# Fast-weight attention: the key-value read is solved on its coefficients instead of being held row by row, and the state is turned first

## The chip, the cores and the metric

The kernel runs on one core of one Trainium2 chip. The metric is the device time of the whole program in microseconds (us). A core has five engines with queues of their own: TensorE (PE, matmuls and transposes), VectorE (DVE), ScalarE (ACT), GpSimd (POOL) and SyncE (SP, which here only issues transfers). Each runs its instructions in the order in which they are written; semaphores are the only thing that orders one engine against another.

## The reference

A small language-model tower on 16 sequences of 128 tokens. In order: an embedding with a decayed memory and four MLP layers (`tok`), a fast-weight attention (`L0_attn`), a mixture of experts, a second attention and a second mixture of experts. The change lies in the fast-weight attention. There the scan runs over the 16 sequences (`slen` = T = 16), 128 tokens are the batch, and there are NH = 8 heads of DH = 32:

```python
def ff_step(W, inp):
    qt, kt, vt, bt = inp
    v_old = jnp.einsum('bhij,bhj->bhi', W, kt)
    W = W + (bt * (vt - v_old))[..., :, None] * kt[..., None, :]
    z = jnp.einsum('bhij,bhj->bhi', W, qt)
    return (W, z)
...
def rec_step(carry, inp):
    R, h = carry
    zt, kt, vt, bt = inp
    q_rec = jax.nn.softmax(h, axis=-1)
    v_old = jnp.einsum('bhij,bhj->bhi', R, kt)
    R = R + (bt * (vt - v_old))[..., :, None] * kt[..., None, :]
    h = zt + jnp.einsum('bhij,bhj->bhi', R, q_rec)
    return ((R, h), h)
```

The first scan (`fast`) has no feedback from its output to its queries; the second (`rec`) has: the query of step t is the softmax of the state h of step t - 1.

## The kernel before

The kernel never forms W or R. It keeps the vectors u_r = b_r (v_r - v_old) of every row r and reads with dot products: z_t is the sum over r <= t of (k_r . q_t) u_r, and u_t needs the sum over r < t of (k_r . k_t) u_r. A stage ahead (`grams`) computes all dot products on PE and moves them by DMA into `C` (SBUF tile `coefs`): for step t, entries 0 to NH-1 are the key coefficients of the fast half, NH to 2NH-1 those of the recurrent half, 2NH to 3NH-1 the query coefficients of the fast half. `UV[:, r, 0]` and `UV[:, r, 1]` hold the vectors of the two halves, 256 elements each (8 heads of 32).

The stage that matters here starts when `C` is complete. Its 16 steps are written out by hand, engine by engine:

- POOL: `row_scale(t)` (scales the coefficients and the values of row t, both halves), `held(t)` (products of the key coefficients of row t with all u_r, r < t, both halves at once, two rows in a piece), `queries(t - 1)` (products of query coefficients with u_r for a part of the rows). Four buffers each for the held and the query products.
- PE: sums such products by accumulating transposes against the identity (`turned_sum`, 128 columns of the 256 at a time): `held(t + 1)` into `held_sum`, `turn_held` turns that sum back, and `read_out` and `queries` add the products of both reads into `h_bank(t)`. `turn_state(t)` turns the finished state back to tokens in rows, `out_projection(t)` applies the output matrix.
- ACT: `held_out(t)` saves the held sum, `state(t)` saves the state to `hsT`, `exponentials(t)` is the exponential of the query softmax, `query_row(t)` copies query coefficients into PSUM.
- DVE: `query_sub(t)` (maximum and subtraction on the turned state, lines L1781 and L1783), `read_coefficients(t)` (dot products of the softmaxed state with the recurrent keys, L1797 to L1816), `products` (L1774: coefficients times u_r for up to four rows; `fast` for the first read, `rec` for the second), `out_add`, `update(t + 1)` (L1761: u = scaled value minus held sum).

A step on DVE is `query_sub(t)`, the second half of the fast products, `read_coefficients(t)`, the rec products, `out_add(t - 1)`, `update(t + 1)` and the first half of the fast products of step t + 1 (there are two halves from step 8 on; rows 4 to 7 and 12 to 15 of the fast read are POOL's). The next `query_sub` waits for the state to come back: DVE's rec products, PE `read_out`, ACT `state`, PE `turn_state`. Semaphores of note: `held_p`/`held_mm` and `query_p`/`query_mm` (POOL's products made and summed), `read_p`/`read_mm` (DVE's), `upd_done` (rows of `UV` that are final), `h_T` (state turned).

## Time and profile before

| | us |
|---|---|
| median of 3 runs | 729.44 (727.9 to 730.09) |
| the profiled execution | 727.95 |
| span of the profiled execution | 726.2 |
| the stage of the 16 steps, with the DMA wait ahead of it | about 257 to 484 of the span |

A profile row says where an engine was busy, and in brackets how long it had been idle and what released it. Matmul records are modelled at their ends, and PE's clock stands in rows as a share of full speed: 1.00 is 2.4 GHz, 0.50 is 1.2 GHz.

### The profile page before, as it was taken

How to read it: one execution, taken by the hardware profiler on the slowest of the kernel's cores; microseconds unless marked ns; L12 is line 12 of the kernel's file. 1: busy time of each engine (PE TensorE's matmuls, PEld its weight loads, DVE VectorE, ACT ScalarE, POOL GpSimd, SP SyncE). 2: the span in 40 equal slices, each digit the busy share in tenths (PEclk: the TensorE clock that was granted, in tenths of full speed). 3: DMA queues.
4: the chain of work that ended last, by engine and by line, in shares of the span. 5: the costliest groups of instructions: out<-in, count | busy, mean ns of one | idle time of the engine just before them, and what ended most of it. 6: DMA issues, size and time to landing. Idle time of an engine off the chain costs nothing.

```text
span 726.2 us, 12294 instructions
## 1 busy us (share of the span) xinstructions
PE 600.5 (83%) x4657; PEld 473.8 (65%) x4657; DVE 444.4 (61%) x1099; ACT 277.9 (38%) x500; POOL 361.0 (50%) x402
## 2 busy tenths in 40 slices
PE   6889999998987706876887778666999698899996
PEld 3657777685556605766786767553688587785776
DVE  3644343337667736889789999985443726663534
ACT  0075354437976611211110100023733436566550
POOL 1696242217208636889889999346553300001334
PEclk9999999999999965889899999978998769999999
DMA  7000000000004330000000000000000000000000
GB/s 247 1 1 1 2 1 0 1 1 1 0 1 80 74 84 21 1 1 1 0 2 1 1 0 1 1 1 1 1 1 1 1 1 2 1 2 1 6 11 14
DMA packets 10698, 10.35 MB, mean 14 GB/s; under 512 B 5904, under 2 KB 9680, under 8 KB 10384
## 3 DMA queue, kind: packets, MB, share of 16 engines
q1 hardware_dynamic: 7936, 7.54, 3.7%
q0 software_dynamic: 1984, 1.62, 1.2%
q8 instruction: 37, 0.61, 0.4%
q10 hardware_dynamic: 720, 0.41, 0.2%
q14 instruction: 21, 0.17, 0.1%
HBM read 5.70 MB, written 0.52 MB: 9 GB/s over the span
## 4 chain that ended last, share of the span: by engine, by line
PE 56%; DVE 24%; ACT 7%; issue 5%; DMA 3%; POOL 3%; SPq 2%; ACTq 0%; DVEq 0%; POOLq 0%
PE bank L1071 8%; PE bank L1059 7%; DVE features L1774 6%; DVE bank L1808 5%; PE bank L1148 5%; DVE features L1797 5%; PE bank L1359 4%; PE bank L1322 4%; PE bank L1357 3%; PE bank L1423 2%; PE bank L1139 2%; PE bank L1411 2%; PE bank L1108 2%; PE bank L1117 2%; SPq L379 2%
## 5 line engine op out<-in xcount | busy, mean ns | idle before, releaser
L1148 PE MATMUL bank<-ident,features 128*128 128x128 f32 x920 | 127.0, 298 | 65.2 <-DVE features L1774 38.8
L1148 PEld LDWEIGHTS bank<-ident,features 128*128 128x128 f32 x920 | 114.0, 155 | 75.5 <-DVE features L1774 47.4
L506 POOL TENSOR_TENSOR features<-UV,coefs 128x1024 f32<-128x1024 f32 (+1 forms) x64 | 117.4, 1857 | 17.8 <-PE bank L1148 9.2
L1774 DVE TENSOR_TENSOR features<-UV,bank 128x1024 f32<-128x1024 f32 (+3 forms) x64 | 66.2, 1065 | 0.9
L695 ACT ACTIVATE G<-bank,cols 128x512 f32<-128x512 f32 x64 | 43.3, 686 | 49.6 <-PE bank L1059 49.6
L1059 PE MATMUL bank<-xs,weights 128*128 128x512 f32 x128 | 60.0, 614 | 2.5 <-ACT xs L686 2.5
L1071 PE MATMUL bank<-weights,G 128*128 128x128 f32 x512 | 59.8, 276 | 0.0
L1071 PEld LDWEIGHTS bank<-weights,G 128*128 128x128 f32 x512 | 58.4, 192 | 0.0
L349 POOL TENSOR_SCALAR rstd<-mv 128x4 f32<-128x4 f32 x8 | 1.9, 237 | 112.2 <-DVE mv L361 112.2
L762 ACT ACTIVATE hsT<-bank 128x256 f32<-128x256 f32 x16 | 6.1, 383 | 102.0 <-PE bank L1148 102.0
L481 POOL TENSOR_TENSOR UV<-xs,rows 128x512 f32<-128x512 f32 x16 | 20.3, 1270 | 46.8 <-DVE xs L1672 46.7
L1139 PE MATMUL bank<-features 32*128 32x136 f32 x768 | 33.8, 312 | 10.3 <-DVE sx L1723 2.5
L1797 DVE TENSOR_TENSOR features<-RK,bank 128x1024 f32<-128x1024 f32 (+3 forms) x40 | 41.8, 1045 | 0.1
L1059 PEld LDWEIGHTS bank<-xs,weights 128*128 128x128 f32 x128 | 24.0, 198 | 27.4 <-issue 24.3
L1808 DVE TENSOR_REDUCE bank<-features 128x32 f32<-128x1024 f32 (+3 forms) x40 | 41.5, 1058 | 0.0
L1139 PEld LDWEIGHTS bank<-features 32*128 32x128 f32 x768 | 28.7, 205 | 15.5 <-issue 4.3
L2095 DVE TENSOR_REDUCE RK<-bank 128x4 f32<-128x512 f32 x32 | 21.9, 684 | 26.0 <-PE bank L1411 26.0
L1672 DVE TENSOR_TENSOR xs<-bank,UV 128x512 f32<-128x512 f32 x16 | 11.1, 692 | 41.0 <-PE bank L1071 38.1
L340 POOL TENSOR_SCALAR rstd<-mv 128x4 f32<-128x4 f32 x32 | 7.7, 240 | 56.8 <-DVE mv L361 55.5
L342 POOL TENSOR_TENSOR rstd<-rstd,neghalf 128x4 f32<-128x4 f32 x32 | 33.2, 1037 | 2.7
L664 POOL TENSOR_TENSOR features<-features 128x512 f32<-128x512 f32 (+2 forms) x21 | 17.1, 816 | 27.1 <-DVE features L2188 17.1
L373 DVE TENSOR_SCALAR UV<-xs,mv,rstd 128x128 f32<-128x128 f32 x48 | 13.4, 343 | 24.6 <-POOL rstd L342 24.6
(318 smaller groups left out, 1346.2 us busy)
## 6 DMA issues: line engine op xcount, KB each, us to landing
weights<-in_w SPq DMA_DIRECT2D x2, 1024.0 KB, 11.6
features<-in_tok SPq DMA_DIRECT2D x1, 768.0 KB, 5.9
weights<-in_ew SPq DMA_DIRECT2D x4, 128.0 KB, 3.0
weights<-in_ew SPq DMA_DIRECT2D x2, 256.0 KB, 2.8
coefs<-G SPq DMA_DIRECT2D x16, 25.5 KB, 3.4
rows<-in_rows SPq DMA_DIRECT2D x1, 384.0 KB, 6.6
out_h<-H SPq DMA_DIRECT2D x3, 128.0 KB, 2.0
coefs<-G POOLq DMA_DIRECT2D x14, 25.5 KB, 4.9
```

The costliest lines, as they stand in the source:

```text
L342: pool.tensor_tensor(rstd[:, k, 0:n], rstd[:, k, 0:n], neghalf[:, 0:n], ALU.pow).then_inc(s["ln_rstd"], 1)
L506: pool.tensor_tensor(out, u, co, ALU.mult).then_inc(s["held_p"], 1)
L695: act.activation(G[:, 4 * (w % 2) + f, :], up_bank(f)[:], ACT.Gelu, bias=col("b1", 4 * i + f)).then_inc(s["tok_gelu"], 1)
L1059: mm(up_bank(f)[:], w1[:, i, P * f:P * f + P], xT[:, w % 2, :], start=True, stop=True).then_inc(s["tok_up"], 1)
L1071: last = mm(down_bank(w)[:, DT * j:DT * j + DT], G[:, 4 * (w % 2) + f, P * j:P * j + P], w2[:, i, f, :], start=(f == 0), stop=(f == 3))
L1139: last = mm(bank[4 * k + j][:, GB * SL * n:GB * SL * n + GB * SL], feat[left + k][x, g, 0:T].rearrange("p s b -> p (s b)"), feat[right + k ...
L1148: last = mm(out[:, P * k:P * k + P], x[:, P * k:P * k + P], ident[:], is_transpose=True, start=first and k == 0, stop=last_ and k == n - 1 ...
L1322: mm(expert_bank(k, c, e)[:], ew1[k][r, e // 2, :], xin(k, c)[r], start=True, stop=True).then_inc(s[f"x_up{e % 2}"], 1)
L1359: last = mm(bank[4 + t % 2][:, D * e:D * e + D], g, ew2[1][:, e, :], start=True, stop=True)
L1774: dve.tensor_tensor(out, u, co.unsqueeze(3).broadcast_to([P, R, NH, DH]), ALU.mult)\
L1797: ch(dve.tensor_tensor(PD[:, j, 0:R * HB].rearrange("p (r x) -> p r x", r=R), RK[:, r0:r1_, :], e.unsqueeze(1).broadcast_to([P, R, HB]), A ...
L1808: ch(dve.tensor_reduce(bankCR[:, r0:r1_, :], PD[:, j, 0:(r1_ - r0) * HB].rearrange("p (r h j) -> p r h j", r=r1_ - r0, h=NH), AX_X, ALU.add))
```

## The change

The fast half's u_r are no longer formed. Since its queries don't depend on its outputs, the triangular system can be solved on the coefficients: `weigh_keys` scales the key coefficients of a block of rows, `eliminate` subtracts, for one row x after the other from the last to the first, (query coefficient of x) times (key coefficients of row x) from the query coefficients of rows below x, and `weigh_reads` scales the result. The fast read is then a sum over the raw values `UV[:, r, 0]`. It is done in blocks of CH = 4 steps: steps 0 to 3 on DVE (in step 0), steps 4 to 15 on POOL by the table `SOLVE`, which spreads the eliminations over POOL's steps 1 to 10. `row_scale`, `held`, `held_out`, `turn_held` and `update` deal with the recurrent half alone, and a held piece is now four rows of 256 elements instead of two of 512. DVE makes the fast products of rows 0 to 3 only, POOL all others. The order changes on every engine: PE turns the state right behind the rec read-out, POOL makes the queries of the same step, DVE does `out_add` behind `query_sub` and the whole fast product of the next step ahead of it. `expert_bias`, two products for the next stage, moves from steps 1 and 3 to steps 13 and 14 of POOL.

```diff
-READS = [x for x in read_pieces() if x[0] == "rec" or x[2] % 8 == 0]
-QUERIES = [x for x in read_pieces() if x[0] == "fast" and x[2] % 8]
-HELDS = [(t, r0, r1) for t in range(1, T) for r0, r1 in pieces(t, 2)]
+READS = [x for x in read_pieces() if x[0] == "rec" or x[2] == 0]
+QUERIES = [x for x in read_pieces() if x[0] == "fast" and x[2]]
+HELDS = [(t, r0, r1) for t in range(1, T) for r0, r1 in pieces(t)]
...
+        def weigh_keys(eng, lo, hi):
+
+            x = C[:, lo:hi, 0:NH, 0:hi]
+            return eng.tensor_tensor(x, x, bsum2[:, lo:hi, 0].unsqueeze(3).broadcast_to([P, hi - lo, NH, hi]), ALU.mult)
+
+        def eliminate(eng, ch, lo, hi, x, scratch):
+
+            t0 = max(lo, x)
+            n = hi - t0
+            full = [P, n, NH, x]
+            less = scratch[:, 0:n * NH * x].rearrange("p (t h r) -> p t h r", t=n, h=NH)
+            cq = C[:, t0:hi, 2 * NH:KD * NH, 0:x]
+            ch(eng.tensor_tensor(less, C[:, t0:hi, 2 * NH:KD * NH, x].unsqueeze(3).broadcast_to(full),
+                                 C[:, x, 0:NH, 0:x].unsqueeze(1).broadcast_to(full), ALU.mult))
+            ch.settle()
+            ch(eng.tensor_tensor(cq, cq, less, ALU.subtract))
+
+        def weigh_reads(eng, ch, lo, hi):
...
+            ch(eng.tensor_tensor(cq, cq, rsum[:, lo:hi, 2, :].unsqueeze(3).broadcast_to(full), ALU.mult))
+            ch.settle()
+            eng.tensor_tensor(cq, cq, bsum[:, 0:hi, 0, :].rearrange("p r h -> p h r").unsqueeze(1).broadcast_to(full),
+                              ALU.mult).then_inc(s["query_scaled"], 1)
...
+            SOLVE = {1: (("rows", 4, 8), ("less", 4, (7, 6, 5))),
+                     2: (("less", 4, (4, 3, 2, 1)), ("done", 4, 8)),
+                     3: (("rows", 8, 16), ("less", 8, (11, 10, 9, 8))),
+                     4: (("less", 8, (7, 6, 5, 4)),),
+                     5: (("less", 8, (3, 2, 1)), ("done", 8, 12), ("less", 12, (15, 14))),
+                     6: (("less", 12, (13, 12, 11)),),
+                     7: (("less", 12, (10, 9, 8)),),
+                     8: (("less", 12, (7, 6, 5)),),
+                     9: (("less", 12, (4, 3)),),
+                     10: (("less", 12, (2, 1)), ("done", 12, 16))}
...
             for t in range(1, T):
...
-                held(t)
-                queries(t - 1)
-                if t in (1, 3):
-                    expert_bias(t // 2)
-            queries(T - 1)
+                held(t)
+                queries(t)
+                if t == 1:
                     pool.wait_ge(s["sums_done"], 2)
+                if t in SOLVE:
+                    solve(SOLVE[t])
+                if t in (13, 14):
+                    expert_bias(t - 13)
...
             for t in range(T):
+                read_out("fast", t, reads_of("fast", t))
+                queries(t)
                 if t + 1 < T:
                     held(t + 1)
-                second_half(t)
-                if t + 1 < T:
                     turn_held(t + 1)
-                queries(t)
                 read_out("rec", t, reads_of("rec", t))
                 if t + 1 < T:
-                    first_half(t + 1)
                     turn_state(t)
                     out_projection(t)
...
             def next_query(t):
 
                 update(t)
-                dve.wait_ge(s["upd_done"], t + 1)
                 dve.wait_ge(s["query_row"], t + 1)
-                part = reads_of("fast", t)
-                products("fast", t, part[0:len(part) // 2])
+                products("fast", t, reads_of("fast", t))
 
             def step(t):
                 if t:
                     query_sub(t)
-                part = reads_of("fast", t)
-                products("fast", t, part[len(part) // 2:])
+                    out_add(t - 1)
                 read_coefficients(t)
+                dve.wait_ge(s["upd_done"], t + 1)
                 products("rec", t, reads_of("rec", t))
-                if t:
-                    out_add(t - 1)
                 if t == 0:
+                    first_reads()
                     normalisers(slice(CH, T))
-                if t == 1:
                     ch.settle()
                     strengths(slice(CH, T))
-                if t >= 2 and t + 2 < 2 * CH - 1:
-                    query_scale(t - 1)
                 if t + 1 < T:
                     next_query(t + 1)
```

Where the order moves, first on PE, step 12 of the stage. `bank<-ident,features` are the transposes that sum products (of `held`, of the fast read and of the rec read, all kept in `features`), `bank<-ident,G` those of POOL's queries, `bank<-ident,accT` is `turn_held`, `bank<-ident,hsT` is `turn_state`. Before, with 52 for `held(13)` and 8 for half of the fast read in the first row, and 26 for the rec read and 8 for the first half of step 13 in the fourth:

```order
L1148 MATMUL bank<-ident,features 128x128 x60
L1168 MATMUL bank<-ident,accT 128x128 x4
L1148 MATMUL bank<-ident,G 128x128 x10
L1148 MATMUL bank<-ident,features 128x128 x34
L1187 MATMUL bank<-ident,hsT 128x128 x2
L1195 MATMUL bank<-outw,hsT 128x64 x2
```

and of the change:

```order
L1205 MATMUL bank<-ident,features 128x128 x8
L1205 MATMUL bank<-ident,G 128x128 x18
L1205 MATMUL bank<-ident,features 128x128 x26
L1225 MATMUL bank<-ident,accT 128x128 x2
L1205 MATMUL bank<-ident,features 128x128 x26
L1244 MATMUL bank<-ident,hsT 128x128 x2
L1252 MATMUL bank<-outw,hsT 128x64 x2
```

The 26 of the rec read now stand directly ahead of `turn_state`, and the transposes of a step fall from 116 to 84.

On POOL, from `row_scale(7)` up to `row_scale(8)`. `features<-UV,coefs` is `held`, `G<-UV,coefs` is `queries`, `coefs<-coefs,bsum` and `UV<-UV,coefs` are `row_scale`. Before:

```order
L488 TENSOR_TENSOR coefs<-coefs,bsum 128x16x7
L490 TENSOR_TENSOR UV<-UV,coefs 128x512
L506 TENSOR_TENSOR features<-UV,coefs 128x1024 x3
L506 TENSOR_TENSOR features<-UV,coefs 128x512
L520 TENSOR_TENSOR G<-UV,coefs 128x768
```

and of the change, where `xs<-coefs` and `coefs<-coefs,xs` are the two operations of an `eliminate`:

```order
L514 TENSOR_TENSOR coefs<-coefs,bsum 128x8x7
L516 TENSOR_TENSOR UV<-UV,coefs 128x256
L532 TENSOR_TENSOR features<-UV,coefs 128x1024
L532 TENSOR_TENSOR features<-UV,coefs 128x768
L545 TENSOR_TENSOR G<-UV,coefs 128x1024
L388 TENSOR_TENSOR xs<-coefs 128x320
L391 TENSOR_TENSOR coefs<-coefs,xs 128x4x8x10
L388 TENSOR_TENSOR xs<-coefs 128x288
L391 TENSOR_TENSOR coefs<-coefs,xs 128x4x8x9
L388 TENSOR_TENSOR xs<-coefs 128x256
L391 TENSOR_TENSOR coefs<-coefs,xs 128x4x8x8
```

Two held products are gone, and six small products stand between the queries and the next row's `row_scale`.

On DVE, from behind the last rec product of step 12 to the start of step 13's coefficients. Before:

```order
L1857 TENSOR_TENSOR H<-bank,H 128x64
L1761 TENSOR_TENSOR UV<-UV,bank 128x512
L1774 TENSOR_TENSOR features<-UV,bank 128x1024
L1781 TENSOR_REDUCE mx<-bank 128x8
L1783 TENSOR_TENSOR dd<-bank,mx 128x256
L1774 TENSOR_TENSOR features<-UV,bank 128x1024
L1797 TENSOR_TENSOR features<-RK,bank 128x1024
```

and of the change:

```order
L1809 TENSOR_TENSOR UV<-UV,bank 128x256
L1822 TENSOR_TENSOR features<-UV,bank 128x1024
L1829 TENSOR_REDUCE mx<-bank 128x8
L1831 TENSOR_TENSOR dd<-bank,mx 128x256
L1899 TENSOR_TENSOR H<-bank,H 128x64
L1845 TENSOR_TENSOR features<-RK,bank 128x1024
```

The product between `dd` and the coefficients (L1797, now L1845) is gone, and `out_add` stands there.

## Rows read from the trace of the kernel before

**Rows 1.** Window of the stage: PE, PEld, DVE, ACT, POOL busy, clock, DMA:

```profile
257.00:484.00 227.00, 157.99 (x1176) 142.70 (x1177) 187.70 (x293) 25.73 (x63) 171.55 (x120) 0.86 0.03 8
```

**Rows 2.** Waits of DVE in the stage (us in total, times, longest us):

```profile
DVE mx L1781 <- PE bank L1187: 21.5, 15, 2.1
```

**Rows 3.** Timeline, coefficients of step 12 to coefficients of 13: start, us, engine, line:

```profile
411.43 1.21 DVE L1797 TENSOR_TENSOR features<-RK,bank 128x1024 f32<-128x1024 f32 x1
...
419.70 3.81 DVE L1774 TENSOR_TENSOR features<-UV,bank 128x1024 f32<-128x1024 f32 x4
420.97 3.57 PE L1148 MATMUL bank<-ident,features 128*128 128x128 f32 x26 [1.90 <-DVE features L1774]
...
424.58 0.38 ACT L762 ACTIVATE hsT<-bank 128x256 f32<-128x256 f32 x1 [7.47 <-PE bank L1148]
...
425.55 1.09 PE L1148 MATMUL bank<-ident,features 128*128 128x128 f32 x8 [1.01 <-DVE features L1774]
...
426.90 0.42 DVE L1781 TENSOR_REDUCE mx<-bank 128x8 f32<-128x256 f32 x1 [1.40 <-PE bank L1187]
427.09 4.54 PE L1148 MATMUL bank<-ident,features 128*128 128x128 f32 x40
...
428.83 1.21 DVE L1797 TENSOR_TENSOR features<-RK,bank 128x1024 f32<-128x1024 f32 x1
```

**Rows 4.** Timeline of DVE, ends of steps 6, 7 and 8 and what follows:

```profile
331.81 2.09 DVE L1774 TENSOR_TENSOR features<-UV,bank 128x1024 f32<-128x1024 f32 x2
...
335.88 0.42 DVE L1781 TENSOR_REDUCE mx<-bank 128x8 f32<-128x256 f32 x1 [1.26 <-PE bank L1187]
...
343.12 2.35 DVE L1774 TENSOR_TENSOR features<-UV,bank 128x1024 f32<-128x1024 f32 x2
...
349.53 0.42 DVE L1781 TENSOR_REDUCE mx<-bank 128x8 f32<-128x256 f32 x1 [2.07 <-PE bank L1187]
...
350.87 1.22 DVE L1797 TENSOR_TENSOR features<-RK,bank 128x1024 f32<-128x1024 f32 x1
...
356.85 2.68 DVE L1774 TENSOR_TENSOR features<-UV,bank 128x1024 f32<-128x1024 f32 x3
...
363.39 0.42 DVE L1781 TENSOR_REDUCE mx<-bank 128x8 f32<-128x256 f32 x1 [1.87 <-PE bank L1187]
```

**Rows 5.** Windows of 2 us, PE busy and its granted clock:

```profile
312.00:314.00 2.00, 1.80 (x9) 0.50 0.00 0
...
474.00:476.00 2.00, 0.00 (x0) 0.50 0.00 0
```

**Rows 6.** Timeline, read-outs at the low clock, steps 4 and 15:

```profile
310.13 1.55 DVE L1774 TENSOR_TENSOR features<-UV,bank 128x1024 f32<-128x1024 f32 x2
...
315.10 0.42 DVE L1781 TENSOR_REDUCE mx<-bank 128x8 f32<-128x256 f32 x1 [2.09 <-PE bank L1187]
...
475.94 4.61 DVE L1774 TENSOR_TENSOR features<-UV,bank 128x1024 f32<-128x1024 f32 x4
477.21 6.05 PE L1148 MATMUL bank<-ident,features 128*128 128x128 f32 x32 [8.19 <-DVE features L1774]
...
483.30 0.38 ACT L762 ACTIVATE hsT<-bank 128x256 f32<-128x256 f32 x1 [17.88 <-PE bank L1148]
```

**Rows 7.** Groups of POOL by shape, count | busy, mean ns | idle before:

```profile
L506 POOL TENSOR_TENSOR features<-UV,coefs 128x1024 f32<-128x1024 f32 x56 | 108.9, 1968 | 11.2 <-PE bank L1148 6.2 <-DVE UV L1761 5.0
...
L520 POOL TENSOR_TENSOR G<-UV,coefs 128x256 f32<-128x256 f32 x2 | 1.3, 634 | 0.0
...
L488 POOL TENSOR_TENSOR coefs<-coefs,bsum 128x240 f32<-128x240 f32 x1 | 0.6, 596 | 0.0
...
L488 POOL TENSOR_TENSOR coefs<-coefs,bsum 128x16 f32<-128x16 f32 x2 | 0.4, 222 | 10.1 <-DVE bsum L1745 10.1
```

**Rows 8.** DVE around the first step, and step 4's start:

```profile
272.15 1.95 DVE L1739 RECIPROCAL coefs<-coefs 128x288 f32<-128x288 f32 x1
...
304.52 0.42 DVE L1781 TENSOR_REDUCE mx<-bank 128x8 f32<-128x256 f32 x1 [1.00 <-PE bank L1187]
```

80 lines of the change are left out of this document (47 added, 33 removed).

## The prediction, on record before the changed kernel ran

> **What bounds the kernel now.** Only one stretch of the program is touched, so I first read the windows by stage: the 16 steps take 227 us with the DMA wait ahead of them, and in them DVE is busy for 188 us, POOL for 172 us and PE for 158 us [rows 1]. No engine is full, so the next view is the waits of DVE: 21.5 us in 15 waits, one per step, for the transposed state to come back from PE [rows 2]. The timeline of one step says what a step consists of [rows 3]. DVE's last rec product of step 12 ends at 423.51 (419.70 + 3.81), `query_sub` of step 13 starts at 426.90 and the coefficients of step 13 (L1797) start at 428.83. I call 423.51 to 426.90 the exit of a step (3.39 us) and 426.90 to 428.83 its entry (1.93 us). Between an entry and the next exit DVE is busy without a gap in `read_coefficients` and the rec products, and there the change alters nothing. So a step's time is entry + fixed work + exit, as long as POOL's held sum is there in time, and the change is to be judged by entries, exits and POOL.
>
> **What the change does to the entry.** The entry is maximum, subtraction and the fast product of 1.13 us (the start of the next instruction; the row says 1.21), so 0.80 us without it. The coefficients also wait for ACT's exponential. Step 8 shows that wait bare, since its product is only one row long: 1.34 us from 349.53 to 350.87 [rows 4]. After the change `out_add` (0.22 us) stands in that wait, so every entry is 1.34 us: 0.6 us less in steps 1 to 7 and 11 to 15, and in steps 8, 9 and 10, whose product is one, two and three rows long, 0, 0.1 and 0.3 us less. `out_add` costs nothing there; without the wait it would cost 0.14 us.
>
> **What it does to the exit.** At step 12 ACT saves the state at 424.58, 1.07 us after DVE's end, then PE must wait for the first half of the next fast read (1.01 us idle, 1.09 us of transposes from 425.55) before it turns the state [rows 3]. The changed order puts the turn directly behind the rec read. Step 6, which has no first half yet, shows such an exit: 333.90 to 335.88, 2.0 us [rows 4]. The update (0.34 us for half of its columns) and the fast product (1.13 us) fit into it. So 3.4 us become 2.0 us, if PE is at its full clock. Steps 4 and 15 show the price if it isn't. Step 4: 311.68 to 315.10, 3.4 us [rows 6], at a granted clock of 0.50 [rows 5]. Step 15: 32 transposes take 6.05 us from 477.21, and the state is taken 2.75 us after DVE's end at 480.55 [rows 6]; with the save, the turn and their hops (0.95 us, what step 6 has between) that is an exit of 3.7 us.
>
> **Which clock PE will have.** Before step 15's read-out PE had been idle for 8.2 us and the clock was 0.50 [rows 5, 6]; before step 12's it had been idle for 1.9 us after dense work and it was fast, 26 transposes in 3.6 us [rows 3]. At full clock 40 transposes take 4.54 us, 0.113 us each [rows 3]. In the changed step 12 PE has 8 + 18 + 26 = 52 of them, 5.9 us; with 0.5 us for turn and projection and 0.9 us for the save and turn of the held sum it is done 7.3 us after the step's start. The first rec product is ready after entry, coefficients (411.43 to 419.70, 8.3 us [rows 3]) and one product, 1.34 + 8.3 + 1.2 = 10.8 us. The idle stretch grows from 1.9 us to about 3.5 us, in steps 9 to 14 alike (3.0 to 3.8), because the held sums have half the transposes. Between the row of 1.9 us (fast) and that of 8.2 us (slow) I take the slow one as likelier: steps 7 and 8 too went slow, and there the end of the rec read was late, 345.47 to 349.53 is 4.1 us and 359.53 to 363.39 is 3.9 us, 0.5 to 0.7 us over step 12's exit [rows 3, 4]. So I take the exits of steps 4, 5 and 9 to 15 at the low clock. The Trainium skill, "TensorE: Matmul & The Clock Gate", section "A second HAM failure mode: psum-queue depth-cycling", says that short idles between groups of matmuls can make the clock swing; the trace shows both, a fast read-out behind 1.9 us of idle and slow ones. By that rule the sum below stands near 722; by the row of 1.9 us it would be 708.
>
> **POOL's sum.** Its prices: 1.97 us for a product of 1024, 0.63 for one of 256 (1.945 and 0.59 from start to start), and for small ones 0.222 us at 16 elements and 0.596 at 240 [rows 7], so 0.195 us + 1.67 ns per element; each that waits for the one ahead of it gets 0.08 us. An elimination of n elements is two of these. By `SOLVE` and the sizes in the order's rows steps 1 to 7 hold 58 such instructions with 11,500 elements: 58 x 0.275 + 11,500 x 0.00167 = 35.1 us, by step 3.3, 4.7, 6.6, 4.6, 6.4, 5.2, 4.5. Steps 8 to 10 add 9.1 us. Against that, held products fall from 120 rows of 512 to 120 of 256 elements, `row_scale` from about 1.4 us to 0.8. What a step of POOL costs (queries, solve, next row's scaling, next held) is 5.1, 7.0, 9.3, 8.5, 11.2, 10.9 and 11.2 us for steps 1 to 7, then 11.5, 10.7, 13.4, 10.6, 11.8, 14.6, 15.6. It starts at 276.8: DVE's reciprocal, at 272.15 before [rows 8], comes behind eight small products of `first_reads` (1.8 us by POOL's nearest row of 0.22 us [rows 7], having none of DVE that small beside it), and 1.95 + 0.8 us of reciprocal and strengths follow. So held(8) is complete at 276.8 + 63.2 = 340.0.
>
> DVE over the same steps, at 1.93 to 1.34 us entries. Steps 2 and 3 are POOL's: held(4) is complete at 276.8 + 21.4 = 298.2; PE sums it (8 transposes at 0.22 us, 1.8), ACT saves it and PE turns it (1.2), then come the 8 transposes of rec(3) (1.8), and save and turn of the state (1.2): step 4 starts at 304.2, where it started at 304.52 [rows 8]. The late start from `first_reads` is made good by the shorter held(2). From there on POOL is 3 to 4.5 us ahead of DVE's exits, not more: step 7's exit starts at 344.2 (345.47 less 0.3 and four entries of 0.6, more 1.4 for a slow exit of step 5, all from the sum below) and held(8) is there at 340.0, with 2.3 to 4 us of sum, save and turn to do. It is hidden, but only just, and each further us on POOL in steps 1 to 7 would show.
>
> **The sum.** Up to step 4: 0.3 us gained. Steps 4 to 7: four entries of 0.6 (2.4), step 7's exit 4.1 to 2.0 (2.1), step 5's exit 2.0 to 3.4 at the low clock, since POOL gives PE nothing for 6.4 us of its solve (-1.4): 3.1. Step 8: exit 3.9 to 2.0, 1.9 gained, as POOL's products keep PE busy right up to the read. Steps 9 to 14: exits of 3.7 instead of 3.4 (3.5 and 3.6 in 9 and 10, with fewer rows), entries 0.1, 0.3 and four times 0.6: 2.8 - 1.5 = 1.3. Step 15: entry 0.6, same end. Together 7.2 us. The profiled execution took 727.95, 1.75 us more than its span of 726.2, and nothing outside the stage changes, so 720.8; the median of the runs is 1.5 us above it, so 722.2 on that basis. I say 722.
>
> Not in the sum: `expert_bias` in steps 13 and 14 (3.8 us, hidden behind 1.6 us or more of room per step and no longer in the way of steps 1 and 3), `query_scale` gone from DVE (it lay in the exit's wait), ACT's save of 256 instead of 512 columns (in the term of the held sum).
>
> **Rivals.** *The clock stays up* (0.15). If 3.5 us of idle don't bring it down, exits in steps 4, 5 and 9 to 14 are 2.0 us and step 15's end 1.7 us shorter: 1.4 + 1.4 + 3.1 + 6.8 + 1.7 = 14.4 more, 708. For it: the idle before step 12's read was over half of that without any fall. Against it: steps 7 and 8. Mixed cases lie between.
>
> *Everything eaten* (0.16). The clock is low in steps 6 to 8 too (three times 1.4 us) or POOL is 10% dearer, and 7 us shrink to 0 to 3: 726.5 to 729.5.
>
> *POOL becomes the bound of steps 2 to 9, and the kernel slower* (0.11). The small eliminations have three free dimensions with strides and repeats, which no row shows at this size; from below they can't be under 0.22 us, from above the nearest row is that of 1024 at 1.9 ns per element, and in between lies doubt. A solve that costs half more makes held(8) complete at 357.5; with 4.6 us of sums, turns and read-out step 8 starts near 362, 12.6 us later than before, of which steps 9 to 15 give back 2 to 4: 738. It decides from about 8 us more on POOL up to step 7, 23% of 35.1. The Trainium skill, "GPSIMD Engine Reference", section "Elementwise — side-by-side cycle accounting", gives 4497 ns for 2048 elements, 2.2 ns per element where this trace has 1.9 or less at 1024. By its figure the solve up to step 7 would be some 6 us longer (an estimate from that page), and the sum would come to about 727.
>
> *The main case* (0.58): gain of 3 to 12 us, 717 to 726.
>
> **The numbers.** 0.3% (2.2 us) is about what a measurement of this kernel can tell from no change. Faster: the main case nearly whole and the high clock, 0.73. Same: most of the third case, 0.15. Slower 0.12. The range leaves out the far half of the first rival and the bound by POOL: 712 to 729.
>
> **What the profile should show.** Eliminations on POOL near 0.2 + 1.67 ns per element, one of 224 at 0.57 us. Entries of 1.34 us. `turn_state` directly behind the save, and exits of 2.0 or 3.4 to 3.7 us going with a granted clock of 1.00 or 0.50 in the read-out. PE idle for 3 to 4 us ahead of the rec read in steps 9 to 14. DVE never waiting for the held sum from step 4 on. The stage ending near 476 where it ended at 483.30. What would prove me wrong: a DVE wait at `update` after step 4, eliminations that take over 0.7 us each, or full clock throughout.

## The result: 722.2 us, and where the 6.5 us come from

The changed kernel takes 722.17 us (median of 4 runs, 720.68 to 722.83), the kernel before 728.67 us beside it (4 runs, 727.9 to 730.09): ratio 0.9906, 95% interval 0.9881 to 0.993. The forecast was 722.0. The size is right, but the profile shows that it came from terms that are partly wrong and cancel. (One traced execution, that of experiment 9, took 1035.56 us at a mean granted clock of 0.559; its exits aren't read, and that experiment's ratio comes from the five other executions.)

The profiled execution of the changed kernel took 722.83 us with a span of 721.1 us. Its window of the stage and DVE's waits in it, to be set beside [rows 1, 2]:

```profile
261.00:482.00 221.00, 136.68 (x904) 121.68 (x904) 175.77 (x289) 20.26 (x63) 159.51 (x173) 0.78 0.03 8
```

```profile
DVE mx L1829 <- PE bank L1244: 20.1, 14, 2.4
...
DVE UV L1809 <- PE bank L1225: 8.1, 4, 2.8
```

PE has some 270 transposes fewer, and its mean granted clock in the window fell from 0.86 to 0.78. DVE's wait for the turned state is almost what it was, 20.1 us after 21.5. The other wait of DVE on PE grew: four times it stands at `update` for the held sum, 8.1 us in all, the last time ahead of step 6. Before, that wait was about half as long, the last ahead of step 2:

```profile
DVE UV L1761 <- PE bank L1168: 4.4, 2, 3.3
```

The same step as [rows 3], coefficients of step 12 to coefficients of 13:

```profile
411.54 1.22 DVE L1845 TENSOR_TENSOR features<-RK,bank 128x1024 f32<-128x1024 f32 x1 [0.32 <-ACT bank L832]
...
419.81 3.81 DVE L1822 TENSOR_TENSOR features<-UV,bank 128x1024 f32<-128x1024 f32 x4
421.09 5.40 PE L1205 MATMUL bank<-ident,features 128*128 128x128 f32 x26 [3.94 <-DVE features L1822]
423.54 0.41 DVE L1809 TENSOR_TENSOR UV<-UV,bank 128x256 f32<-128x256 f32 x1
423.87 1.21 DVE L1822 TENSOR_TENSOR features<-UV,bank 128x1024 f32<-128x1024 f32 x1
...
426.52 0.38 ACT L818 ACTIVATE hsT<-bank 128x256 f32<-128x256 f32 x1 [9.86 <-PE bank L1205]
426.96 0.44 PE L1244 MATMUL bank<-ident,hsT 128*128 128x128 f32 x2 [0.47 <-ACT hsT L818]
...
427.43 0.42 DVE L1829 TENSOR_REDUCE mx<-bank 128x8 f32<-128x256 f32 x1 [2.35 <-PE bank L1244]
...
428.23 0.21 DVE L1899 TENSOR_TENSOR H<-bank,H 128x64 f32<-128x64 f32 x1
428.77 1.22 DVE L1845 TENSOR_TENSOR features<-RK,bank 128x1024 f32<-128x1024 f32 x1 [0.32 <-ACT bank L832]
```

Entry: 427.43 to 428.77, 1.34 us where it was 1.93. Turn: directly behind the save of the state. Exit: 423.62 (419.81 + 3.81) to 427.43, 3.81 us where it was 3.39. The 26 transposes of the rec read took 3.57 us before and take 5.40 us now, behind 3.94 us of idle instead of 1.90. The windows say why:

```profile
422.00:424.00 2.00, 2.00 (x11) 2.00 (x11) 2.00 (x5) 0.00 (x0) 1.96 (x2) 0.50 0.00 0
...
430.00:432.00 2.00, 2.00 (x21) 2.00 (x19) 2.00 (x3) 0.00 (x0) 2.00 (x2) 1.00 0.03 8
```

PE is busy throughout both windows, and gets 11 matmuls done at 0.50 (1.2 GHz), 21 at 1.00 (2.4 GHz). The turn-first order should have saved 1.4 us here; the low clock took it.

Cutting the stage at the starts of `query_sub` (from the first DVE instruction on the coefficients to the last save of the state) gives 216.15 us before (267.15 to 483.30) and 210.88 us after (270.79 to 481.67), so 5.3 us. I use this stage length below, because what lies outside it moved by up to 10 us between profiled executions of these kernels (505 to 515 us), with next to nothing changed there. No kernel's stage was traced twice, so how far a stage length repeats isn't known; entries and fixed work agree to 0.02 us from kernel to kernel, exits go with the clock.

### The profile page after: what moved, and what is told of

The parts are those of the page before. It is cut to its first block, busy times and chain, and to the rows that moved or that the text cites. A ratio compares the mean times of both kernels' runs of the same rounds, so it can differ in the third digit from the quotient of the medians.

```text
span 721.1 us, 11767 instructions
## 1 busy us (share of the span) xinstructions
PE 575.3 (80%) x4387; PEld 449.8 (62%) x4387; DVE 434.7 (60%) x1098; ACT 272.6 (38%) x500; POOL 349.2 (48%) x455
## 4 chain that ended last, share of the span: by engine, by line
PE 56%; DVE 17%; POOL 9%; ACT 8%; DMA 4%; issue 3%; SPq 3%; ACTq 0%; POOLq 0%; DVEq 0%
PE bank L1128 8%; PE bank L1116 7%; PE bank L1205 6%; DVE features L1845 4%; DVE bank L1856 4%; PE bank L1368 4%; PE bank L1405 4%; PE bank L1403 3%; SPq L405 3%; PE bank L1469 2%; PE bank L1165 2%; POOL features L532 2%; PE bank L1457 2%; PE bank L1174 2%; DVE features L1822 2%
## 5 line engine op out<-in xcount | busy, mean ns | idle before, releaser
L1205 PE MATMUL bank<-ident,features 128*128 128x128 f32 x628 | 102.3, 328 | 70.9 <-DVE features L1822 52.2
L1205 PEld LDWEIGHTS bank<-ident,features 128*128 128x128 f32 x628 | 91.7, 174 | 76.9 <-DVE features L1822 40.0
L532 POOL TENSOR_TENSOR features<-UV,coefs 128x1024 f32<-128x1024 f32 (+3 forms) x36 | 59.4, 1670 | 4.1 <-DVE UV L1809 4.0
L1822 DVE TENSOR_TENSOR features<-UV,bank 128x1024 f32<-128x1024 f32 (+3 forms) x56 | 58.1, 1073 | 0.7 <-ACT bank L826 0.2
L1845 DVE TENSOR_TENSOR features<-RK,bank 128x1024 f32<-128x1024 f32 (+3 forms) x40 | 41.9, 1046 | 4.8 <-ACT bank L832 4.8
L545 POOL TENSOR_TENSOR G<-UV,coefs 128x1024 f32<-128x1024 f32 (+3 forms) x24 | 39.1, 1646 | 7.2 <-PE bank L1205 7.2
```

The costliest lines, as they stand in the source:

```text
L532: pool.tensor_tensor(out, u, co, ALU.mult).then_inc(s["held_p"], 1)
L545: pool.tensor_tensor(out, u, co, ALU.mult).then_inc(s["query_p"], 1)
L1205: last = mm(out[:, P * k:P * k + P], x[:, P * k:P * k + P], ident[:], is_transpose=True, start=first and k == 0, stop=last_ and k == n - 1 ...
L1822: dve.tensor_tensor(out, u, co.unsqueeze(3).broadcast_to([P, R, NH, DH]), ALU.mult)\
L1845: ch(dve.tensor_tensor(PD[:, j, 0:R * HB].rearrange("p (r x) -> p r x", r=R), RK[:, r0:r1_, :], e.unsqueeze(1).broadcast_to([P, R, HB]), A ...
```

## The experiments

Each time is a median of 6 to 12 runs (5 for the dealt-out kernel), beside the kernel before on the same chip (728.1 us in the first four experiments, 730.1 in the next four, 728.5 in the next three, 727.7 in the last). Exits and entries are read from DVE's timeline as in the prediction; stages come from the one traced execution of each kernel, medians from all.

**1. The old kernel with nothing but the turn moved.**

```diff
                 read_out("rec", t, reads_of("rec", t))
                 if t + 1 < T:
-                    first_half(t + 1)
                     turn_state(t)
                     out_projection(t)
+                    first_half(t + 1)
```

> The kernel before with one thing moved: PE turns the state and projects it ahead of the read-out of the next step's first half. Theory (the exits carry the gain): exits of steps 10 to 14 go from 3.4 us to 2.0 us with the clock high as before, those of 7 to 9 by 0.2 to 0.7 us with the clock low, together about 8 us less: 720.5, as fast as the whole change or faster. Rival (the gain comes from the solve and the halved held sums, the turn was hidden by DVE's own update and product): no change, 728 to 729.

Measured: 717.88 us, ratio 0.9888 (0.984 to 0.9935), stage 205.85 us. Two lines moved give at least as much as the whole change: the medians are 4.3 us apart and the stages 5.0, while the intervals of the two ratios overlap. PE at the read of step 10, before and here:

```profile
387.77 2.88 PE L1148 MATMUL bank<-ident,features 128*128 128x128 f32 x22 [2.57 <-DVE features L1774]
391.75 1.09 PE L1148 MATMUL bank<-ident,features 128*128 128x128 f32 x8 [1.10 <-DVE features L1774]
392.68 0.38 PE L1187 MATMUL bank<-ident,hsT 128*128 128x128 f32 x2
```

```profile
385.57 2.88 PE L1148 MATMUL bank<-ident,features 128*128 128x128 f32 x22 [1.31 <-DVE features L1774]
388.92 0.44 PE L1187 MATMUL bank<-ident,hsT 128*128 128x128 f32 x2 [0.47 <-ACT hsT L762]
...
389.59 0.61 PE L1148 MATMUL bank<-ident,features 128*128 128x128 f32 x4
```

The read itself takes 2.88 us in both; what goes is the 1.10 us of idle and 1.09 us of transposes ahead of the turn. Exits of steps 7 to 13 are 1.90 to 2.32 us. The transposes that moved behind the turn also shorten the idle ahead of the next read (1.31 us for 2.57 in step 10). In step 8 the clock goes with it. The read, first with the eight transposes behind it and then without, before and here:

```profile
358.12 5.01 PE L1148 MATMUL bank<-ident,features 128*128 128x128 f32 x26 [2.08 <-DVE features L1774]
```

```profile
359.37 2.44 PE L1148 MATMUL bank<-ident,features 128*128 128x128 f32 x18 [1.22 <-DVE features L1774]
```

The granted clock from 360 to 362 us was 0.50 before and 1.00 here. Exits of steps 7, 8 and 9 fell by 1.96, 1.88 and 1.59 us, where I had expected 0.2 to 0.7 with the clock low as before.

**2. The changed kernel without that move**: the solve on coefficients alone.

```diff
+                if t == 0:
+                    read_out("fast", t, reads_of("fast", t))
-                read_out("fast", t, reads_of("fast", t))
                 queries(t)
...
                 if t + 1 < T:
+                    read_out("fast", t + 1, reads_of("fast", t + 1))
                     turn_state(t)
```

> The changed kernel with the turn put back behind the read-out of the next step's fast rows. Theory: each exit of steps 3 to 14 is 1.0 to 1.3 us longer, so 12 to 15 us more, about 735, slower than the kernel before. Rival (turn hidden): within 2 us of the changed kernel, 722 to 724.

Measured: 729.71 us, ratio 1.005 (1.0013 to 1.0087), stage 218.58 us: slightly slower than before, and half way between my theory (735) and the rival (722 to 724). The move costs 7.7 us of stage and not 12 to 15, since many exits of the changed kernel were slow already. Together with experiment 1 this is a square of four:

```
time (stage), us         old solve          solve on coefficients
old order                728.7 (216.15)     729.7 (218.58)
state turned first       717.9 (205.85)     722.2 (210.88)
```

The reorder is worth 7.5 and 10.8 us in the two columns. The solve on coefficients costs 1 us in one row and 4 us in the other (2.4 and 5.0 us of stage), although entries are shorter. The next two experiments look for what it costs.

**3. Dummy transposes.** The changed kernel with transposes of the identity into an unused part of a PSUM bank, in TensorE's idle time: behind the queries of steps 3, 5, 6 (16, 20, 8 of them) and behind `turn_held` in steps 9 to 14 (20) and 15 (60).

```diff
+            def keep_busy(n):
+                for _ in range(n):
+                    nc.tensor.transpose(held_sum[:, 384:512], ident[:], ident[:])
...
                     turn_held(t + 1)
+                keep_busy(IDLE_LATE.get(t, 0))
                 read_out("rec", t, reads_of("rec", t))
```

> The changed kernel with transposes of the identity into unused columns of the held sum's bank, where PE would idle: 16, 20 and 8 behind the queries of steps 3, 5 and 6, 20 behind turn_held in steps 9 to 14, 60 in step 15. They compute nothing. Theory (the exits are long because the granted clock is 0.50 in the read-out): clock 1.00 in these read-outs, exits of 9 to 14 from 2.8 to 3.9 us down to 2.0 us and the end of step 15 1.7 us earlier, together 9 to 11 us less: 711 to 713. Rival (the exits are long for another reason, such as the late held sum or ACT): 722 or more, by up to 2 us for the added work.

Measured: 708.99 us, ratio 0.9772 (0.9721 to 0.9822), stage 203.11 us. The read of step 12:

```profile
410.14 2.35 PE L1329 MATMUL bank<-ident 128*128 128x128 f32 x20
414.25 3.58 PE L1205 MATMUL bank<-ident,features 128*128 128x128 f32 x26 [1.76 <-DVE features L1832]
418.30 0.44 PE L1244 MATMUL bank<-ident,hsT 128*128 128x128 f32 x2 [0.47 <-ACT hsT L818]
```

26 transposes in 3.58 us instead of 5.40, with 2.35 us of work that computes nothing put ahead of them. Exits of steps 9 to 13 are 1.89 to 2.10 us, and the granted clock in them is 1.00: the theory. The 13.2 us between the medians are more than this clock is worth, though. The stage lost 7.8 us: steps 9 to 15 gave 9.0 us, the size expected, and steps 0 to 8 cost 1.2, with exits of 3.42, 3.12, 5.49, 3.73 and 3.33 us in steps 4 to 8 and six waits at `update` (8.7 us). Of the other 4.9 us of the traced executions 3.8 lie ahead of the stage, where the kernels are the same. Idle time right ahead of a read isn't all that counts either: step 14's read, behind 1.97 us of idle, still took 5.16 us for 30 transposes.

**4. No eliminations.** The changed kernel without the rank-one updates on POOL (its output leaves the solve's triangular part out).

```diff
-            SOLVE = {1: (("rows", 4, 8), ("less", 4, (7, 6, 5))),
+            SOLVE = {1: (("rows", 4, 8),),
...
```

> The changed kernel without the eliminations on POOL (the rows and done parts of the solve stay, so the fast reads of steps 4 to 15 lack their corrections). Theory: POOL is late in steps 1 to 7 by about what DVE waits at its update (2.8, 1.1, 1.8 and 2.5 us ahead of steps 2, 3, 4 and 6); without 34 us of eliminations these waits shrink to the turn of the held sum, 4 to 6 us less, 716 to 718. Rival (the solve is hidden, the waits come from PE's low clock): 721 to 722.

Measured: 716.57 us, ratio 0.9839 (0.9784 to 0.9894), stage 202.55 us. DVE never waits at `update`; exits of steps 1 to 7 are 1.88 to 2.98 us instead of 1.99 to 5.26, and step 8 starts 71.9 us after the stage's start instead of 81.2. Exits of steps 8 to 13 are 3.2 to 4.0 us, much as in the changed kernel (3.0 to 3.9). So POOL's lateness (9 us in steps 1 to 7) and the low clock of the later reads are two separate costs.

**5. The eliminations dealt out again**: the same ones, placed where POOL has room.

```diff
-                     2: (("less", 4, (4, 3, 2, 1)), ("done", 4, 8)),
-                     3: (("rows", 8, 16), ("less", 8, (11, 10, 9, 8))),
-                     4: (("less", 8, (7, 6, 5, 4)),),
-                     5: (("less", 8, (3, 2, 1)), ("done", 8, 12), ("less", 12, (15, 14))),
-                     6: (("less", 12, (13, 12, 11)),),
-                     7: (("less", 12, (10, 9, 8)),),
...
+                     2: (("less", 4, (4, 3, 2, 1)),),
+                     3: (("done", 4, 8), ("rows", 8, 12), ("less", 8, (11,))),
+                     4: (("less", 8, (10, 9, 8)),),
+                     5: (("less", 8, (7, 6, 5, 4)),),
+                     6: (("less", 8, (3, 2, 1)), ("rows", 12, 16), ("less", 12, (15,))),
+                     7: (("done", 8, 12), ("less", 12, (14, 13))),
...
```

> The changed kernel with its eliminations dealt out again over the steps: GpSimd's load goes from steps 1 to 3 and 5 into steps 4, 6, 7 and 11, the sum of the work unchanged. Theory A (half of what the solve part costs is GpSimd's lateness: DVE waited 2.46 us at the update ahead of step 6 and 4.75 and 4.32 us exits stand at steps 1 and 3): those exits fall to 2 to 3 us, the stage is 2 to 5 us shorter, and the time is 717 to 720 us. Theory B (the lateness is hidden behind the low clock's cold transposes, which the same exits would pay anyway): the waits at the updates go, exits stay, 721 to 723 us.

Measured: 717.88 us, ratio 0.9854 (0.9815 to 0.9893), stage 205.56 us. DVE's waits in the stage:

```profile
DVE mx L1830 <- PE bank L1245: 20.4, 14, 2.5
...
DVE UV L1810 <- PE bank L1226: 2.8, 1, 2.8
```

8.1 us of waiting for held sums have become 2.8, one wait, at step 1, and the stage is 5.3 us shorter: theory A in time and for step 3 (exit 4.32 to 2.31 us), not for step 1, whose exit stayed at 4.74. The exits of steps 3 and 5 alone gave 5.3 us. Beside them steps 4 and 7 lost 3.0 us to reads at a low clock, and steps 8 to 13 gave 2.2 us that no theory had. The solve part now costs nothing (717.9 against 717.9 in experiment 1), and gives nothing either.

**6. Both cures together**: dealt out, and dummy transposes in steps 3 to 15 (10 to 14 behind the queries of steps 3 to 8; 6 to 24 behind `turn_held` in 7 to 14 and 66 in 15).

> The same dealt-out eliminations with dummy transposes on TensorE in its idle time in steps 3 to 15. Theory A (clock and GpSimd's lateness are two costs that add): the 14 us that dummy transposes alone gave and the gain of dealing out, together 704 to 707 us, exits of steps 4 to 14 all near 2 us. Theory B (with the clock up, steps are shorter and GpSimd has less time to each, so it becomes late elsewhere): 708 to 711 us with update waits of over 1 us in steps 5 to 9.

Measured: 706.12 us, ratio 0.9694 (0.9654 to 0.9735), stage 196.40 us. Theory A. Three exits stayed at 3.3 us (steps 4, 6 and 8).

**7 and 8. The same for the old solve.** Experiment 7 is experiment 1 with 6 to 10 dummy transposes ahead of the rec read in steps 4 to 14 and 60 in step 15. Experiment 8 is experiment 1 with `out_add` placed behind `query_sub` for steps 1 to 7 and the one fast product of these steps made ahead of the step:

```diff
                 if t:
                     query_sub(t)
+                if t and t < 2 * CH:
+                    out_add(t - 1)
...
-                if t:
+                if t >= 2 * CH:
                     out_add(t - 1)
```

> The kernel before with the state turned first and dummy transposes ahead of the recurrent read's, 6 to 10 in steps 4 to 14 and 60 in step 15. The old order turned first already has exits of 1.9 to 2.3 us in steps 7 to 13, so little is left to win: Theory A (the clock is what the dummies give back, and here it costs only the exits 5, 6, 14 and the last read-out): 713 to 716 us. Theory B (the dummies delay the read's own transposes as much as they save): 717 to 719 us.

> The kernel before with the state turned first, and for steps 1 to 7 the single full-inverse product made wholly ahead of the step, and the output's addition moved behind the query's subtraction. Theory A (the changed kernel's short entry of 1.34 us in steps 2 to 7 comes from what stands on DVE between subtraction and exponential, and not from the rank-one form): entries of steps 2 to 7 fall from 1.93 to about 1.4 us, and the time is 3 to 4 us under the kernel with the state turned first, 714 to 715 us. Theory B (what leaves the entry goes into the exit, one product of up to 1 us longer ahead of the query): 717 to 720 us.

Measured: 714.26 us, ratio 0.9796 (0.9753 to 0.984), stage 205.96 us; and 719.44 us, ratio 0.9846 (0.9793 to 0.9899), stage 205.09 us. For experiment 7 that is theory A's range, for experiment 8 theory A's entry and theory B's time. Step 5 in experiment 8:

```profile
315.06 0.42 DVE L1782 TENSOR_REDUCE mx<-bank 128x8 f32<-128x256 f32 x1
315.51 0.42 DVE L1784 TENSOR_TENSOR dd<-bank,mx 128x256 f32<-128x256 f32 x1
315.85 0.21 DVE L1860 TENSOR_TENSOR H<-bank,H 128x64 f32<-128x64 f32 x1
316.39 1.22 DVE L1798 TENSOR_TENSOR features<-RK,bank 128x1024 f32<-128x1024 f32 x1 [0.32 <-ACT bank L775]
```

The entry is 1.33 us with the old solve as well: for steps 2 to 7 the short entry is a matter of where two instructions stand. But it did not shorten the program. The stage lost 0.8 us where six entries lost 3.3: the exits of steps 1 to 4 grew by 2.2 us (7.17, 2.90, 2.19, 2.08 to 8.41, 3.05, 2.67, 2.37), those of steps 1 and 2 with waits at `update` for POOL's held sum (3.71 and 0.76 us, where experiment 1 has 3.33 and none). A shorter step early in the stage only reaches POOL sooner. Another 1.3 us went in step 15, whose read was at 0.50 here. The medians (719.4 and 717.9, runs from 710.9 to 722.7) tell no difference. Experiment 7's dummies brought 4 us in the medians, and none in the profiled stage: exits 6, 14 and 15 gave 2.6 us, and exit 13 (4.90 us for 2.32) ate them. Step 13 ran into POOL:

```profile
413.09 13.57 POOL L506 TENSOR_TENSOR features<-UV,coefs 128x1024 f32<-128x1024 f32 x7
```

```profile
426.72 3.45 PE L1148 MATMUL bank<-ident,features 128*128 128x128 f32 x16 [0.84 <-POOL features L506]
```

The seven held products of 512 elements a row take 13.6 us of a step of 16 to 17, PE's sum ends at 430.2, and the read, whose first product was ready at 429.2, starts at 432.81 behind turn, queries and dummies. In experiment 1 POOL's products take as long, but the same 16 transposes don't:

```profile
429.89 1.97 PE L1148 MATMUL bank<-ident,features 128*128 128x128 f32 x16 [0.83 <-POOL features L506]
```

So of the 2.6 us by which exit 13 grew, 1.5 are slower transposes, in spite of dummies in every step, and 1.0 are the eight dummies themselves. With the solve on coefficients the same products are half as long.

**9. Both for the old solve**: experiment 8 with 10 to 16 dummy transposes in steps 4 to 14 and 64 in step 15.

> The old form of the solve, state turned first, short entries in steps 2 to 7, and dummy transposes ahead of the recurrent read's in steps 4 to 15. It is the counterpart, without the solve on coefficients, of the dealt-out changed kernel with dummy transposes (706.1 us). Theory A (the solve on coefficients is worth what its rows show once clock and GpSimd's lateness are gone: step 1's exit 4.75 against 7.5 to 8.4 us, and entries of steps 11 to 15 0.6 us shorter): 710 to 713 us. Theory B (everything that the solve part gives can be had by other means, and the two meet): 706 to 708 us.

Measured: 714.7 us, ratio 0.9817 (0.9781 to 0.9852). It stands 8.6 us above experiment 6, and the intervals of the ratios are apart. Both theories put it too low; A is the nearer. One placement of dummies was tried for the old solve with short entries, so how much of the 8.6 us another would win back isn't known.

**10. More dummies** in experiment 6, in steps 4 to 8 ahead of the rec read.

```diff
-            IDLE_LATE = {7: 6, 8: 8, 9: 18, 10: 20, 11: 22, 12: 22, 13: 24, 14: 24, 15: 66}
+            IDLE_LATE = {4: 10, 5: 6, 6: 10, 7: 12, 8: 18, 9: 18, 10: 20, 11: 22, 12: 22, 13: 24, 14: 24, 15: 66}
```

> The dealt-out changed kernel with dummy transposes, with 6 to 18 of them also behind the held sum's turn in steps 4 to 8, where TensorE stood idle for 1.4 to 1.5 us ahead of the recurrent read's transposes and then ran them at 0.50 to 0.59 of its clock. Theory A (those idle times are what lowers the clock of the exits): exits of steps 4, 6 and 8 fall from 3.3 to about 2 us, 702 to 704 us. Theory B (the clock there follows from the whole step's light load, and the idle time just ahead does not matter): exits stay, 705 to 707 us.

Measured: 705.93 us, ratio 0.9696 (0.9662 to 0.9729), stage 195.92 us. The read of step 4:

```profile
308.75 1.25 PE L1330 MATMUL bank<-ident 128*128 128x128 f32 x10
...
310.46 1.31 PE L1206 MATMUL bank<-ident,features 128*128 128x128 f32 x10 [0.45 <-DVE features L1833]
```

It took 2.39 us in experiment 6, behind 1.54 us of idle:

```profile
310.92 2.39 PE L1206 MATMUL bank<-ident,features 128*128 128x128 f32 x10 [1.54 <-DVE features L1833]
```

Exits of steps 4, 6 and 8 fell to 1.99, 1.88 and 1.99 us, as theory A has it. But the time is the same, in theory B's range, since exits 10 and 11 grew (2.95 and 4.69 us, with 1.88 and 2.10 in experiment 6). These aren't slow transposes; step 11 shows what it is:

```profile
389.16 3.62 PE L1206 MATMUL bank<-ident,features 128*128 128x128 f32 x16 [0.84 <-POOL features L532]
393.25 0.44 PE L1226 MATMUL bank<-ident,accT 128*128 128x128 f32 x2 [0.47 <-ACT accT L812]
393.53 2.56 PE L1330 MATMUL bank<-ident 128*128 128x128 f32 x22
395.93 2.78 PE L1206 MATMUL bank<-ident,features 128*128 128x128 f32 x24
```

The DVE product that the read needs first was there at 392.7 (391.49 + 1.2). PE was still at the held sum, late by POOL's products and (16 transposes in 3.62 us) the clock, and then ran its 22 dummies, 2.4 us, ahead of a read that was ready. Steps 4 to 9 had become shorter by 4 us, and POOL, which has eliminations in steps 9 to 11, was no longer ahead. So the gain of the early steps was given back, by dummies in a fixed number on an engine that was late; 706 us is where this placement ends.

**11 and 12. The old order again**, with the dealt-out eliminations: as experiment 2's edit on experiment 5, and on experiment 10.

> The changed kernel with its eliminations dealt out again, but with the next step's full-inverse transposes ahead of the state's turn, as before the change. Theory A (what made the solve part alone worthless was that GpSimd's lateness in steps 1 to 7 ate what the entries gave): under the kernel before by 2 to 5 us, 723 to 726 us. Theory B (the low clock in the exits ate it, dealing out changes nothing in the old order): 728 to 731 us.

> The dealt-out changed kernel with dummy transposes (705.9 us), but with the next step's full-inverse transposes put back ahead of the state's turn. Dummy transposes fill 1.5 to 4.5 us of TensorE's idle time in each of steps 3 to 15. Theory A (in the old order too the solve part gave nothing because of the low clock alone: with TensorE idle for 3.6 to 4.5 us its transposes ran at half speed; with the clock up the order costs just its 4 to 8 transposes per exit at about 0.11 us): 711 to 716 us. Theory B (the order itself, clock or no clock, is what costs the 10 us that turning first gave): 716 us or more, 10 us and more above the dealt-out kernel with dummies.

Measured: 731.7 us, ratio 1.0024 (0.9992 to 1.0056), stage 218.07 us, one wait at `update`, of 1.1 us in step 1, as in experiment 2; and 718.38 us, ratio 0.9901 (0.9867 to 0.9934), stage 209.08 us. Dealing out does nothing in the old order: theory B. There was no lateness of POOL to take away, since the reads are at the low clock and DVE comes later to each `update`. (The traced executions are not typical here: 725.68 us in experiment 11, 723.17 in experiment 12, with medians of 731.7 and 718.38.) Step 10 of experiment 11, then step 4 of experiment 12:

```profile
392.27 6.35 PE L1206 MATMUL bank<-ident,features 128*128 128x128 f32 x30 [4.47 <-DVE features L1825]
398.46 0.38 PE L1245 MATMUL bank<-ident,hsT 128*128 128x128 f32 x2
```

```profile
312.52 1.31 PE L1206 MATMUL bank<-ident,features 128*128 128x128 f32 x10 [1.32 <-DVE features L1835]
314.31 1.09 PE L1206 MATMUL bank<-ident,features 128*128 128x128 f32 x8 [0.48 <-DVE features L1835]
315.24 0.38 PE L1245 MATMUL bank<-ident,hsT 128*128 128x128 f32 x2
```

At the full clock the order costs what the rows say: from the start of the eight transposes to the turn it is 0.93 us. Exits are 2.87 us in seven of the steps 3 to 10, where experiment 10 has 1.88 to 2.10 in steps 4 to 9. Times 14 exits that is about 13 us, and 718.4 less 705.9 is 12.5. Step by step it isn't that even: the exit of step 0 alone is 1.7 us longer, and both traces have late or slow reads (steps 10 and 11 in experiment 10; 9 and 11 to 14 in experiment 12, at 0.50 to 0.72). So the time is theory B's: the order itself costs the 10 us and more, with dummies too. Theory A had right what one exit pays at the full clock and its product wrong: 14 times 8 times 0.11 is 12.3 us, which gives 718 and not 711 to 716. The old order with the old solve was never run with dummies, so theory A's other half, that the low clock alone makes the solve part worthless in the old order, stays open.

## Why the prediction was right, and where it wasn't

Stage times by segment, forecast gain and measured gain in us, from `query_sub` to `query_sub`:

```
segment             forecast   measured
up to step 4        0.3        0.7
steps 4 to 7        3.1        0.5
step 8              1.9        0.7
steps 9 to 14       1.3        2.9
step 15             0.6        0.5
stage               7.2        5.3
```

**Entries: right**, 1.33 to 1.34 us in every step, `out_add` in the exponential's cover, fixed work unchanged to 0.02 us. That the entry owes this to the solve part was not shown by it: experiment 8 has it without.

**The turn directly behind the read: right, and it is the whole gain.** The sum gave it 4.0 us (exits of steps 7 and 8); alone it is worth 10.3 us of stage (experiment 1): 3.8 us in steps 7 and 8, 6.8 us in steps 9 to 13, whose reads were at the full clock, and -0.4 us in all the others together. In the changed kernel the exits of steps 9 to 13 are 0.4 us longer than before in all: there the low clock took everything that the turn gave.

**The low clock behind 3 to 4 us of idle: right**, in mechanism and almost in size. PE was idle for 3.5 to 4.2 us ahead of the reads of steps 9 to 14, the clock in them was 0.50 (in steps 10 and 14 it rose to 1.00 before their end), and the exits 2.81 to 3.88 us against my 3.5 to 3.7. The case I weighed against it, 708 us at full clock, is near what experiment 3 measured (709.0), but that is chance: the terms of that case make a stage of 194.6 us, experiment 3 has 203.1, and only experiments 6 and 10 come near (196.4 and 195.9). I had put the longer idle down to the halved held sums, rightly, and not drawn the consequence that this loss is the solve part's: some 270 transposes taken off PE were not free. And the idle time right ahead of a read doesn't tell its clock by itself. Behind shorter idles than these both levels stand side by side: before the change step 6 behind 2.66 us was at 1.00 and step 8 behind 2.08 at 0.50, in experiment 6 step 9 behind 1.53 at 1.00 and step 8 behind 1.43 at 0.50. What decides there stays open.

**"DVE never waiting for the held sum from step 4 on": wrong.** This is the step that failed, within the term of 3.1 us for steps 4 to 7, which measured 0.5. Step 5's exit was 1.9 us longer than its term (5.26 for 3.4), by this wait of 2.46 us; step 6's was 2.0 longer (4.02 for 2.0) without a wait, at 0.50; step 4's was 1.4 shorter. DVE waits for `held(6)` in step 5:

```profile
319.73 2.99 POOL L532 TENSOR_TENSOR features<-UV,coefs 128x1024 f32<-128x1024 f32 x2
...
321.56 1.82 DVE L1822 TENSOR_TENSOR features<-UV,bank 128x1024 f32<-128x1024 f32 x2
321.75 2.82 PE L1205 MATMUL bank<-ident,features 128*128 128x128 f32 x12 [4.09 <-POOL features L532]
```

POOL's products end at 322.72, 0.66 us ahead of DVE's rec products, and PE's 12 transposes for the sum take 2.82 us at the low clock, behind 4.09 us of idle. I had checked POOL against DVE at steps 4 and 8, ends of blocks, and not at 6, where the eliminations of two blocks meet (step 5's row of `SOLVE` has three parts). POOL's total was nearly right: `held(8)` came 65.4 us into its sum where I had 63.2, on this basis at 341.9 for 340.0. Small operations cost a little more than my line gave, 0.62 and 0.63 us at 224 elements for 0.57, and the second product of `weigh_reads` more than the first:

```profile
L391 POOL TENSOR_TENSOR coefs<-coefs,xs 128x224 f32<-128x224 f32 x3 | 1.9, 633 | 0.2
L388 POOL TENSOR_TENSOR xs<-coefs 128x224 f32<-128x224 f32 x3 | 1.9, 621 | 0.1
...
L399 POOL TENSOR_TENSOR coefs<-coefs 128x512 f32<-128x512 f32 x1 | 1.5, 1533 | 0.1
...
L397 POOL TENSOR_TENSOR coefs<-coefs 128x512 f32<-128x512 f32 x1 | 1.1, 1059 | 0.1
```

The Trainium skill, "GPSIMD Engine Reference", section "Elementwise — side-by-side cycle accounting", gives 4497 ns for 2048 elements, by which I had estimated 6 us more for the solve; this trace doesn't agree, with 1968 ns at 1024 elements and 0.62 to 0.63 us at 224, and held(8) came 2.2 us later than my sum, not 6. **The rival "POOL is the bound of steps 2 to 9"** did not come about as told, since its condition was 8 us more on POOL up to step 7; but POOL did bound single steps. Experiment 4 puts 9 us on the eliminations in steps 1 to 7, of which the exits of steps 3 and 5 gave 5.3 back in experiment 5 by placement alone.

**Exits 4 to 8** I had as fast or slow one by one, and three of five were of the wrong kind: 1.99 for 3.4 (step 4), 4.02 for 2.0 (step 6), 3.19 for 2.0 (step 8), the last two at the low clock.

**Steps 9 to 14** gave 1.6 us more than forecast, because their slow exits were on average 3.4 us where the sum had 3.65. That a total within 0.2 us of the median comes out of such terms is luck: +0.4, -2.6, -1.2, +1.6 and -0.1 add up to -1.9. The stage gained 5.3 us and the traced execution 5.1, and the median fell by 6.5, to 722.2, from a kernel before that itself measured 0.8 us lower than the 729.44 I started from.

The fastest kernels measured are experiments 6 and 10, at 706 us. There the solve part is worth having: 8.6 us under the old solve with the same cures (experiment 9), and 10.0 us of stage between experiments 10 and 7. Of these the traces put 6.6 us in entries (15 of 1.34 against 26.75 in all), of which experiment 8 has 3.3 with the old solve too, 2.7 us at step 1 (an exit of 4.76 for 7.50), and 1.4 and 4.0 us in the exits of step 5 and of steps 13 and 14, where the old solve's held products are late; against these stand 3.6 us in steps 10 and 11 and 1.6 in steps 0, 2 and 3 of experiment 10. So what the solve on coefficients gives here is an earlier held(2), shorter entries from step 9 on, and a POOL that isn't the next bound of the long steps.

## What to carry to other kernels

Try each part of a change alone: here two moved lines gave 11 us in the medians and the large part took 4 of them back. Work taken from an engine that waits anyway is not a gain by itself, and on TensorE it was a loss here: with idles of 3.5 us and more ahead of the reads the granted clock was 0.50 just where the chain passes through them. Count the idle ahead of each read before and after. Work that only fills time delays what comes behind it when its engine is late, so it has to be placed by the trace and checked again after each gain. Where a slower engine does the replaced work, check its lead over the chain at every step, not at the ends of blocks, and spread its load by that.

## What was not expected of the hardware

- TensorE work that computes nothing made the program faster: 13 us in the medians (722.2 to 709.0), 7.8 of them in the stage. The clock in a read went with what PE did before it. 26 transposes took 3.58 us behind 20 dummies and 1.76 us of idle, 5.40 us behind 3.94 us of idle.
- The first 50 us of the program ran at either clock. With the same instructions, before, after and in experiment 3:

```profile
0.00:50.00 50.00, 39.76 (x114) 24.57 (x115) 24.24 (x101) 13.68 (x25) 26.70 (x47) 1.00 0.28 90
```

```profile
0.00:50.00 50.00, 36.69 (x101) 22.45 (x102) 23.65 (x96) 12.72 (x23) 26.06 (x47) 0.70 0.28 90
```

```profile
0.00:50.00 50.00, 38.43 (x113) 24.07 (x114) 24.01 (x99) 13.54 (x25) 26.54 (x47) 0.69 0.28 90
```

  The stage started at 267.15, 270.79 and 266.95 us. So the start moved by as much as half of the change's effect without a change ahead of it, but a low clock there doesn't explain that by itself: in experiment 3 it was as low and the start the earliest of the three. What moves it isn't shown. With 505 to 515 us outside the stage, the totals of two single profiles here say nothing about a few microseconds.
- Behind the stage the clock differed too: the window 584 to 594 had 0.50 before and 1.00 after, with 76 and 115 matmuls.
- On GpSimd small products with strides and repeats in three dimensions cost about 0.2 us + 1.9 ns per element (0.63 us at 224, 0.96 us at 384; an estimate from the rows of 32 to 384 elements), little more than plain ones; a product with an operand both repeated and transposed cost 1.53 us at 512 elements, one with an operand repeated alone 1.06.
